# Turning the quantised silu product by DMA instead of on TensorE, with the down projection two tiles behind

## The chip, the cores and the metric

The kernel runs on one core of one Trainium2 chip. The metric is the device time of one execution in microseconds: a median of 1254.67 over three runs (1254.53 to 1255.34). Engines are named as in the profile: PE is TensorE, DVE is VectorE, ACT is ScalarE, POOL is GpSimd, SP is SyncE, which issues DMAs.

## The reference

Input is x (2 x 2048 x 512, fp32) and a context of 2 x 77 x 512. A causal cross-attention block of 16 heads comes first, `x = x + attention(layernorm(x), ctx)`, and then the feed-forward block, the one that is changed:

```
def fp4_quant_dequant(x):                      # blocks of 16 along the last dim
    xb = x.reshape(shape[:-1] + (shape[-1] // BLOCK, BLOCK))
    scale = jnp.maximum(jnp.max(jnp.abs(xb), axis=-1, keepdims=True) / 6.0, 1e-12)
    idx = jnp.searchsorted(_MID, jnp.abs(xb / scale))
    return (_GRID[idx] * jnp.sign(xb) * scale).reshape(shape)
def fp4_linear(x, w): return einsum('bsk,nk->bsn', fp4_quant_dequant(x), fp4_quant_dequant(w))
x = layernorm(x1)
h = silu(fp4_linear(x, w_gate)) * fp4_linear(x, w_up)    # 512 -> 1408
out = x1 + fp4_linear(h, w_down)                          # 1408 -> 512
```

The grid is 0, 0.5, 1, 1.5, 2, 3, 4, 6, with sign.

## The kernel before

All is done in 32 tiles of 128 rows (T = 32). The attention phase runs to about 461 us; it also quantises the weights, and leaves x1 and the turned down weights in DRAM. The feed-forward phase is `feed_forward`, a software pipeline written out by hand: each engine runs its own in-order list, `iteration(a)`, for a = 0 to T + 1, of which 4 to T - 2 are one hardware loop. Engines meet only through semaphores. There is no planner: the order of the lines is the order of the work.

Every matrix is carried as two fp32r parts, high and low, and each product is three matmuls (high x high, high x low, low x high). In iteration a TensorE computes gate and up of tile a in four chunks of 352 columns, each of 12 matmuls (`gate`, `up`), two PSUM banks for each. ScalarE takes silu of a gate chunk, VectorE multiplies it with the up chunk into `hid` (`gate_times_up`, L1188). Up of chunk c may start when the product of chunk c - 2 is made, gate of chunk c when silu of chunk c - 2 is done.

The product of tile a - 1 is quantised in iteration a on VectorE, with one step on ScalarE (class `Quant`): block maximum (L115), scale, its inverse and negated inverse, `divide` into z (L135), `shift` on ScalarE (L141), `make_magic`, `add_magic` (L150), `take_magic` (L155), which leaves grid values in fp32, and `rescale` (L161), which multiplies by the block scales into `hidq`. Between these steps stand the same steps for the input of tile a + 1 (`f.norm_stats` to `f.rescale`, 512 columns). TensorE then turns `hidq` in blocks of 128 x 128, in groups of 4, 4 and 3 (`transpose_hq`, L1096), into `hq_ps`; ScalarE copies each group to `hqh` (`hq_high`, L1155), and VectorE takes the rest to `hql` (`hq_low`, L1194). Both are single buffers of 128 x 11 x 128. `down(a - 1)` (L1099 to 1111) ends TensorE's iteration with 33 matmuls of 512 columns. The first copy of a tile has this wait ahead of it (L1148 to 1150), where t is a - 1:

```
                if g == 0:
                    if reached(t):
                        act.wait_ge(down_done, t)
```

VectorE adds the residual from `d_ps` (`add_residual`, L1201), SyncE stores the tile and loads the x1 rows of a later one (ring of 5). The next tile's input is turned by TensorE (`f.transpose`, L284), copied by ScalarE (`f.high`, L289) and VectorE (`f.low`, L293); gate of chunk 0 waits for both. Tiles 0 and T - 1 are quantised in two parts of 704 columns.

## Time and profile before

| what | value |
|---|---|
| median of three runs | 1254.67 us (1254.53 to 1255.34) |
| the profiled execution, span | 1252.7 us |
| instructions in it | 21798 |
| TensorE busy | 1224.3 us (98%) |
| VectorE busy | 1014.9 us (81%) |
| ScalarE busy | 466.5 us (37%) |
| GpSimd busy | 145.7 us (12%) |
| mean DMA rate | 47 GB/s |

The span runs from the first to the last recorded instruction of the profiled execution; the run's time is some 2 us longer than it. Busy matmul time overlaps: each matmul is listed at about 0.32 us (352 columns) or 0.39 us (512), while the next starts 0.16 or 0.23 us after it. So a cost on TensorE is read from one start to the next, and the other engines' from their durations.

### The profile page before, as it was taken

The numbers are of one execution on the slowest core, as the hardware profiler recorded it, in microseconds if no ns is written. First come the engines' busy times: TensorE is split into PE (matmuls) and PEld (weight loads), VectorE is DVE, ScalarE is ACT, GpSimd is POOL, SyncE is SP. The second block draws the span as 40 slices with busy tenths as digits, with TensorE's granted clock in tenths as the row PEclk, the third lists the DMA queues.
The fourth block names the chain that finished last, engine by engine and source line by source line (L and its number), as shares of the span: only waits on it lengthen the run. The fifth ranks groups of instructions, "written<-read, shape, count | busy, mean of one in ns | idle before, by whom it ended". The sixth has DMA issues, their size and how long they took to land.

```text
span 1252.7 us, 21798 instructions
## 1 busy us (share of the span) xinstructions
PE 1224.3 (98%) x7304; PEld 1119.5 (89%) x7304; DVE 1014.9 (81%) x1842; ACT 466.5 (37%) x1142; POOL 145.7 (12%) x239
## 2 busy tenths in 40 slices
PE   6899999999999989999999999999999999999998
PEld 4688888888888879999999999999999999999997
DVE  6899999989999948886887788688778877886875
ACT  3465656565656532222222232222222222322221
POOL 2011111111111100100100010011001000100100
PEclk9899999999999989999999999999999999999999
DMA  6112121211323242010000000000000100010000
GB/s 233 20 51 76 50 75 51 67 59 59 118 84 126 76 164 89 17 35 17 17 29 21 17 17 33 17 17 17 33 17 17 33 17 17 17 33 17 8 17 17
DMA packets 35666, 59.37 MB, mean 47 GB/s; under 512 B 5447, under 2 KB 11087, under 8 KB 35510
## 3 DMA queue, kind: packets, MB, share of 16 engines
q1 hardware_dynamic: 35638, 59.01, 13.9%
q8 instruction: 16, 0.26, 0.1%
q14 instruction: 12, 0.10, 0.0%
HBM read 36.13 MB, written 22.54 MB: 47 GB/s over the span
## 4 chain that ended last, share of the span: by engine, by line
PE 62%; DVE 1%; issue 0%; ACT 0%; DVEq 0%; ACTq 0%
PE g_ps L170 7%; PE g_ps L171 7%; PE g_ps L172 7%; PE u_ps L170 6%; PE u_ps L172 6%; PE u_ps L171 6%; PE d_ps L1108 6%; PE d_ps L1110 6%; PE d_ps L1109 6%; PE hq_ps L1096 3%; PE xn_ps L284 1%; DVE hql L1194 0%; DVE hquant_z L155 0%; DVE hquant_z L150 0%; DVE y L1201 0%
## 5 line engine op out<-in xcount | busy, mean ns | idle before, releaser
L1188 DVE TENSOR_TENSOR hid<-u_ps,silu 128x352 f32<-128x352 f32 x128 | 66.7, 521 | 142.4 <-PE u_ps L172 142.4
L170 PE MATMUL g_ps<-wguh,xnh 128*128 128x352 f32 x512 | 168.0, 328 | 3.7 <-PEq L299 2.2
L170 PE MATMUL u_ps<-wguh,xnh 128*128 128x352 f32 x512 | 167.3, 327 | 0.0
L171 PE MATMUL g_ps<-wgul,xnh 128*128 128x352 f32 x512 | 165.5, 323 | 0.0
L172 PE MATMUL g_ps<-wguh,xnl 128*128 128x352 f32 x512 | 165.3, 323 | 0.0
L172 PE MATMUL u_ps<-wguh,xnl 128*128 128x352 f32 x512 | 164.8, 322 | 0.0
L171 PE MATMUL u_ps<-wgul,xnh 128*128 128x352 f32 x512 | 164.7, 322 | 0.0
L754 ACT ACTIVATE probs<-s_ps,nsmax 128x77 f32<-128x77 f32 x512 | 114.1, 374 | 119.9 <-DVE nsmax L838 119.9
L1144 ACT ACTIVATE silu<-g_ps 128x352 f32<-128x352 f32 x128 | 58.9, 461 | 253.2 <-PE g_ps L172 253.2
L1108 PE MATMUL d_ps<-wd,hqh 128*128 128x512 f32 x352 | 140.3, 398 | 0.0
L1110 PE MATMUL d_ps<-wd,hql 128*128 128x512 f32 x352 | 137.3, 390 | 0.0
L1109 PE MATMUL d_ps<-wd,hqh 128*128 128x512 f32 x352 | 137.1, 389 | 0.0
L170 PEld LDWEIGHTS g_ps<-wguh,xnh 128*128 128x128 f32 x512 | 96.2, 188 | 5.7 <-issue 2.8
L171 PEld LDWEIGHTS g_ps<-wgul,xnh 128*128 128x128 f32 x512 | 96.3, 188 | 1.1
L171 PEld LDWEIGHTS u_ps<-wgul,xnh 128*128 128x128 f32 x512 | 96.3, 188 | 0.0
L170 PEld LDWEIGHTS u_ps<-wguh,xnh 128*128 128x128 f32 x512 | 96.2, 188 | 0.0
L172 PEld LDWEIGHTS g_ps<-wguh,xnl 128*128 128x128 f32 x512 | 96.2, 188 | 0.0
L172 PEld LDWEIGHTS u_ps<-wguh,xnl 128*128 128x128 f32 x512 | 96.1, 188 | 0.0
L243 POOL TENSOR_TENSOR nmean<-f_mv,minus_one 128x1 f32<-128x1 f32 x32 | 6.1, 190 | 687.1 <-DVE f_mv L238 687.1
L662 PEld LDWEIGHTS o_ps<-vbd,probsT 128*128 128x128 f32 (+1 forms) x640 | 76.5, 191 | 4.4
L1110 PEld LDWEIGHTS d_ps<-wd,hql 128*128 128x128 f32 x352 | 66.1, 188 | 14.4
L1155 ACT ACTIVATE hqh<-hq_ps 128x512 fp32r<-128x512 f32 (+1 forms) x96 | 53.9, 561 | 64.3 <-PE hq_ps L1096 64.3
(128 smaller groups left out, 2618.1 us busy)
## 6 DMA issues: line engine op xcount, KB each, us to landing
xin<-in_x_dram SPq DMA_DIRECT2D x32, 256.0 KB, 2.8
x_dram<-x SPq DMA_DIRECT2D x32, 256.0 KB, 2.0
xin<-x_dram SPq DMA_DIRECT2D x32, 256.0 KB, 2.8
out_dram<-y SPq DMA_DIRECT2D x32, 256.0 KB, 2.0
wd_dram<-wd_out SPq DMA_DIRECT2D x11, 512.0 KB, 3.6
wd<-wd_dram SPq DMA_DIRECT2D x1, 5632.0 KB, 17.1
w_in<-in_L_ffn_w_gate_dram SPq DMA_DIRECT2D x11, 256.0 KB, 2.9
w_in<-in_L_ffn_w_up_dram SPq DMA_DIRECT2D x11, 256.0 KB, 2.9
```

Of the source, the lines that this page charges most:

```text
L170: pe.matmul(out, lh, rh, start=(i == 0), stop=False)
L171: pe.matmul(out, lh, rl, start=False, stop=False)
L172: last = pe.matmul(out, ll, rh, start=False, stop=(i == n - 1))
L662: last = pe.matmul(o_ps[:, half, h0 * VW:(h1 + 1) * VW], probsT[0:rows, i, :], vbd[0:rows, b, half, c, 0:(h1 - h0 + 1) * VW], start=(c == ...
L754: last = act.activation(probs[:, h * CTX:(h + 1) * CTX], s_ps[:, bank, o:o + CTX], ACT.Exp, bias=nsmax[:, h:h + 1], scale=SCALE)
L1096: transposed = pe.transpose(hq_ps[:, g % 2, c - c0, :], hidq[:, c * P:(c + 1) * P], ident[:])
L1108: pe.matmul(d_ps[:], hqh[:, c, :], wd[:, 0, c, :], start=(c == 0), stop=False)
L1109: pe.matmul(d_ps[:], hqh[:, c, :], wd[:, 1, c, :], start=False, stop=False)
L1110: summed = pe.matmul(d_ps[:], hql[:, c, :], wd[:, 0, c, :], start=False, stop=(c == FC - 1))
L1144: act.activation(silu[:, c % 2, :], g_ps[:, c % 2, 0:GU_N], ACT.Silu).then_inc(silu_ready, 1)
L1155: act.activation(hqh[:, c0:c1, :], hq_ps[:, g % 2, 0:c1 - c0, :], ACT.Copy).then_inc(hqh_ready, 1)
L1188: dve.tensor_tensor(hid[:, c * GU_N:(c + 1) * GU_N], u_ps[:, c % 2, 0:GU_N], silu[:, c % 2, :], ALU.mult).then_inc(hid_ready, 1)
```

## The change

The product of tile t, for all tiles but the last, is no longer turned on TensorE. VectorE's last rounding step writes the grid values (exact in bf16) to `hg`; one transposing DMA from SyncE turns `hg` into `hgt`. The block scales (88 per row) are reordered by ScalarE, turned by TensorE in one instruction, copied from PSUM by ScalarE, stored to DRAM, and read back by eight broadcasting DMAs into `scale_wide`. VectorE multiplies `hgt` and `scale_wide` into `hqf`, ScalarE copies that to `hqh`, VectorE takes the difference to `hql`: each is now one instruction of 1408 columns. `down(a - 2)` takes the place of `down(a - 1)`, so the pipeline is one iteration longer. The turn of the next input moves ahead of up of chunk 3, `add_residual` of tile a - 3 moves ahead of the input's block maximum. Tile 0 is quantised whole. The last tile keeps the old way, in two parts, with its high and low parts in the space of the gate weights. GpSimd's own loop becomes the common one, with the same work for each tile. The core of the diff (declarations of semaphores, the signature, and longer runs of lines that only go left out; these stand in the listing above):

```diff
-        hidq = sb("hidq", [P, FF])
+        hqf = sb("hqf", [P, FC, P])
         hqh, hql = sb("hqh", [P, FC, P], F32R), sb("hql", [P, FC, P], F32R)
         y = sb("y", [P, 2, E])
         hquant = Quant(ctx, nc, "hquant", FF)
+        hg = sb("hg", [P, FF], BF16)
+        hgt = sb("hgt", [P, FC, P], BF16)
+        scale_cols = sb("scale_cols", [P, FB])
+        scale_rows = sb("scale_rows", [FB, P])
+        scale_wide = sb("scale_wide", [P, FC, P])
...
+        END = T - 1
+        lasth, lastl = (w[:, 0, 0:FF].rearrange("p (c k) -> p c k", k=P) for w in (k.wguh, k.wgul))
...
+        def looped(t):
+
+            return not isinstance(t, int) or 0 <= t < END
+
+        def is_end(t):
+            return isinstance(t, int) and t == END
+
+        LAST = T + 2
...
+            def scales_out(t):
+                sp.wait_ge(rows_ready, t + 1)
+                sp.dma_start(st_dram.rearrange("b (c k) -> (b c) k", k=P), scale_rows[:]).then_inc(rows_stored, 16)
+
+            def grid_transposed(t):
+                sp.wait_ge(hquant.grid_ready, t + 1)
+                if reached(t):
+                    sp.wait_ge(hqf_ready, t)
+                sp.dma_start_transpose(hgt[:], hg[:]).then_inc(hgt_loaded, 16)
+
+            def scales_in(t):
+                sp.wait_ge(rows_stored, 16 * (t + 1))
+                for b in range(P // BLK):
+                    sp.dma_start(scale_wide[b * BLK:(b + 1) * BLK, :, :].rearrange("p c k -> p (c k)"),
+                                 st_dram[b:b + 1, :].to_broadcast([BLK, FF])).then_inc(wide_loaded, 16)
+
...
...
+            for a in range(T + 3):
+                if looped(a - 1):
+                    scales_out(a - 1)
+                if valid(a - 3):
+                    store(a - 3)
+                    if a - 3 + RING < T:
+                        f.load(sp, a - 3 + RING, x1_t[a - 3 + RING])
+                if looped(a - 1):
+                    grid_transposed(a - 1)
+                    scales_in(a - 1)
...
...
+            def scales_transposed(t):
+                pe.wait_ge(cols_ready, t + 1)
+                if reached(t):
+                    pe.wait_ge(rows_ready, t)
+                pe.transpose(hq_ps[0:FB, 0, 0, :], scale_cols[:], ident[:]).then_inc(rows_done, 1)
+
+            def last_transposed(g):
+                pe.wait_ge(last_ready, 1 if g == 0 else 2)
+                if g < 2:
+                    pe.wait_ge(rows_ready, END)
+                else:
+                    pe.wait_ge(lastl_ready, g - 1)
                 c0, c1 = HQ_GROUPS[g]
                 for c in range(c0, c1):
-                    transposed = pe.transpose(hq_ps[:, g % 2, c - c0, :], hidq[:, c * P:(c + 1) * P], ident[:])
-                transposed.then_inc(hqT_done, 1)
+                    transposed = pe.transpose(hq_ps[:, g % 2, c - c0, :], hquant.z[:, c * P:(c + 1) * P], ident[:])
+                transposed.then_inc(lastT_done, 1)
 
...
+                high, low = (lasth, lastl) if is_end(t) else (hqh, hql)
                 for g, (c0, c1) in enumerate(HQ_GROUPS):
-                    pe.wait_ge(hqh_ready, NG * t + g + 1)
-                    pe.wait_ge(hql_ready, NG * t + g + 1)
+                    if is_end(t):
+                        pe.wait_ge(lasth_ready, g + 1)
+                        pe.wait_ge(lastl_ready, g + 1)
+                    elif g == 0:
+                        pe.wait_ge(hqh_ready, t + 1)
+                        pe.wait_ge(hql_ready, t + 1)
                     for c in range(c0, c1):
-                        pe.matmul(d_ps[:], hqh[:, c, :], wd[:, 0, c, :], start=(c == 0), stop=False)
-                        pe.matmul(d_ps[:], hqh[:, c, :], wd[:, 1, c, :], start=False, stop=False)
-                        summed = pe.matmul(d_ps[:], hql[:, c, :], wd[:, 0, c, :], start=False, stop=(c == FC - 1))
+                        pe.matmul(d_ps[:], high[:, c, :], wd[:, 0, c, :], start=(c == 0), stop=False)
+                        pe.matmul(d_ps[:], high[:, c, :], wd[:, 1, c, :], start=False, stop=False)
+                        summed = pe.matmul(d_ps[:], low[:, c, :], wd[:, 0, c, :], start=False, stop=(c == FC - 1))
...
             def iteration(a):
                 if valid(a):
                     gate(a, 0)
                     up(a, 0)
+                if looped(a - 1):
+                    scales_transposed(a - 1)
+                if valid(a):
                     gate(a, 1)
                     up(a, 1)
                     gate(a, 2)
-                if valid(a):
                     up(a, 2)
-                if valid(a - 1):
-                    transpose_hq(a - 1, 0)
-                if valid(a):
                     gate(a, 3)
...
                 if valid(a + 1):
                     f.transpose(pe, a + 1)
-                if valid(a - 1):
-                    transpose_hq(a - 1, 2)
-                    down(a - 1)
+                if valid(a):
+                    up(a, 3)
+                if is_end(a - 1):
+                    last_transposed(0)
+                    last_transposed(1)
+                if valid(a - 2):
+                    down(a - 2)
+                if is_end(a - 1):
+                    last_transposed(2)
 
...
...
+            def turn_scales(t):
+
+                act.wait_ge(hquant.scale_ready, t + 1)
+                if reached(t):
+                    act.wait_ge(rows_done, t)
+                act.activation(scale_cols[:].rearrange("p (b c) -> p b c", c=FC),
+                               hquant.scale[:].rearrange("p (c b) -> p b c", c=FC), ACT.Copy).then_inc(cols_ready, 1)
+
+            def scale_rows_out(t):
+                act.wait_ge(rows_done, t + 1)
+                if reached(t):
+                    act.wait_ge(rows_stored, 16 * t)
+                act.activation(scale_rows[:], hq_ps[0:FB, 0, 0, :], ACT.Copy).then_inc(rows_ready, 1)
+
+            def hq_high(t):
+                act.wait_ge(hqf_ready, t + 1)
+                if reached(t):
+                    act.wait_ge(down_done, t)
+                act.activation(hqh[:], hqf[:], ACT.Copy).then_inc(hqh_ready, 1)
+
+            def last_high(g):
+                act.wait_ge(lastT_done, g + 1)
                 c0, c1 = HQ_GROUPS[g]
-                act.activation(hqh[:, c0:c1, :], hq_ps[:, g % 2, 0:c1 - c0, :], ACT.Copy).then_inc(hqh_ready, 1)
+                act.activation(lasth[:, c0:c1, :], hq_ps[:, g % 2, 0:c1 - c0, :], ACT.Copy).then_inc(lasth_ready, 1)
 
             def iteration(a):
                 if valid(a + 1) and reached(a):
                     f.centre(act, a + 1)
-                if valid(a - 1):
-                    hquant.shift(act, quantised(a - 1), LAST_PART if split(a - 1) else ALL)
+                if looped(a - 1):
+                    turn_scales(a - 1)
+                    hquant.shift(act, a)
+                if is_end(a - 1):
+                    hquant.shift(act, T + 1, LAST_PART)
                 if valid(a + 1) and reached(a):
                     xquant.shift(act, PIECES + a + 2)
                 if valid(a):
...
+                    silu_of_gate(a, 0)
+                if looped(a - 1):
+                    scale_rows_out(a - 1)
+                if valid(a):
+                    silu_of_gate(a, 1)
+                    silu_of_gate(a, 2)
+                if looped(a - 1):
+                    hq_high(a - 1)
+                if is_end(a):
+                    hquant.shift(act, T, FIRST_PART)
                 if valid(a):
                     silu_of_gate(a, 3)
-                if valid(a - 1):
-                    hq_high(a - 1, 1)
                 if valid(a + 1):
                     act.wait_ge(up_done, GU * (a + 1))
                     f.high(act, a + 1)
-                if valid(a - 1):
-                    hq_high(a - 1, 2)
+                if is_end(a - 1):
+                    for g in range(NG):
+                        last_high(g)
 
...
-            def hq_low(t, g):
-                dve.wait_ge(hqh_ready, NG * t + g + 1)
+            def grid(t):
+
+                dve.wait_ge(hquant.sum_ready, t + 1)
+                if reached(t):
+                    dve.wait_ge(hgt_loaded, 16 * t)
+                dve.scalar_tensor_tensor(out=hg[:], in0=hquant.magic[:], scalar=ULP_FLOOR, in1=hquant.z[:],
+                                         op0=ALU.max, op1=ALU.subtract).then_inc(hquant.grid_ready, 1)
+
+            def hq_full(t):
+                dve.wait_ge(hgt_loaded, 16 * (t + 1))
+                dve.wait_ge(wide_loaded, 16 * (P // BLK) * (t + 1))
+                dve.tensor_tensor(hqf[:], hgt[:], scale_wide[:], ALU.mult).then_inc(hqf_ready, 1)
+
+            def hq_low(t):
+                dve.wait_ge(hqh_ready, t + 1)
+                dve.tensor_tensor(hql[:], hqf[:], hqh[:].bitcast(F32), ALU.subtract).then_inc(hql_ready, 1)
+
+            def last_low(g):
+                dve.wait_ge(lasth_ready, g + 1)
                 c0, c1 = HQ_GROUPS[g]
-                dve.tensor_tensor(hql[:, c0:c1, :], hq_ps[:, g % 2, 0:c1 - c0, :], hqh[:, c0:c1, :].bitcast(F32),
-                                  ALU.subtract).then_inc(hql_ready, 1)
+                dve.tensor_tensor(lastl[:, c0:c1, :], hq_ps[:, g % 2, 0:c1 - c0, :], lasth[:, c0:c1, :].bitcast(F32),
+                                  ALU.subtract).then_inc(lastl_ready, 1)
+
+            def quantise_last(part, done):
+                hquant.block_max(dve, hid[:], part)
+                hquant.block_scale(dve, done, part=part)
+                hquant.invert(dve, done, part=part)
+                hquant.negate(dve, done, part=part)
+                hquant.divide(dve, done, hid[:], part)
+
+            def round_last(part, done):
+                hquant.make_magic(dve, done, part)
+                hquant.add_magic(dve, done, part)
+                hquant.take_magic(dve, done, part)
+                hquant.rescale(dve, done, hquant.z[:], part).then_inc(last_ready, 1)
 
...
-                h, x = valid(a - 1), valid(a + 1) and reached(a)
-                part, done = LAST_PART if split(a - 1) else ALL, quantised(a - 1)
+                h, x = looped(a - 1), valid(a + 1) and reached(a)
+                done = a
                 if h:
-                    hquant.block_max(dve, hid[:], part)
+                    hquant.block_max(dve, hid[:])
                 if x:
                     f.norm_stats(dve, a + 1)
                 if h:
...
+                    if reached(a - 1):
+                        dve.wait_ge(cols_ready, a - 1)
+                    hquant.block_scale(dve, done)
+                    hquant.invert(dve, done)
+                    hquant.negate(dve, done)
+                    hquant.divide(dve, done, hid[:])
+                if is_end(a - 1):
+                    quantise_last(LAST_PART, T + 1)
+                if valid(a - 3):
+                    add_residual(a - 3)
                 if x:
                     f.block_max(dve, a + 1)
                     f.invert(dve, a + 1)
                     f.divide(dve, a + 1)
                 if h:
...
+                    hquant.make_magic(dve, done)
+                    hquant.add_magic(dve, done)
                 if x:
                     xquant.make_magic(dve, PIECES + a + 2)
                 if h:
-                    hquant.take_magic(dve, done, part=part)
+                    grid(a - 1)
                 if x:
                     xquant.add_magic(dve, PIECES + a + 2)
                 if valid(a):
                     gate_times_up(a, 0)
...
                 if x:
                     xquant.take_magic(dve, PIECES + a + 2)
                     f.rescale(dve, a + 1)
                 if valid(a):
                     gate_times_up(a, 1)
-                if split(a):
-                    first = quantised(a, FIRST_PART)
+                    gate_times_up(a, 2)
+                if h:
+                    hq_full(a - 1)
+                    hq_low(a - 1)
+                if is_end(a):
                     dve.wait_ge(hid_ready, GU * a + 2)
...
+                    dve.wait_ge(cols_ready, END)
+                    quantise_last(FIRST_PART, T)
+                    round_last(FIRST_PART, T)
+                if valid(a):
                     gate_times_up(a, 3)
...
                 if valid(a + 1):
                     f.low(dve, a + 1)
-                if valid(a - 1):
-                    hq_low(a - 1, 2)
+                if is_end(a - 1):
+                    round_last(LAST_PART, T + 1)
+                    for g in range(NG):
+                        last_low(g)
                 if valid(a):
                     dve.wait_ge(hid_ready, GU * (a + 1))
```

## Rows read from the trace of the kernel before

**Rows 1.** The page, part 1: busy time of each engine.
```profile
PE 1224.3 (98%) x7304; PEld 1119.5 (89%) x7304; DVE 1014.9 (81%) x1842; ACT 466.5 (37%) x1142; POOL 145.7 (12%) x239
```

**Rows 2.** TensorE's waits, 580 us to the end: us in total, times, longest.
```profile
PE hq_ps L1096 <- DVE hql L1194: 0.7, 1, 0.7
PE hq_ps L1096 <- DVE hidq L161: 0.2, 1, 0.2
```

**Rows 3.** Timeline of TensorE, start of tile 1: start us, us [idle before].
```profile
479.05 0.40 PE L170 MATMUL g_ps<-wguh,xnh 128*128 128x352 f32 x1 [1.52 <-ACT xnh L289]
```

**Rows 4.** Timeline of TensorE, start of tile 31.
```profile
1215.32 0.32 PE L170 MATMUL g_ps<-wguh,xnh 128*128 128x352 f32 x1
```

**Rows 5.** Timeline of VectorE over one tile, 618 to 634.2 us.
```profile
618.48 0.53 DVE L1188 TENSOR_TENSOR hid<-u_ps,silu 128x352 f32<-128x352 f32 x1 [3.21 <-PE u_ps L172]
618.92 0.68 DVE L1194 TENSOR_TENSOR hql<-hq_ps,hqh 128x512 fp32r<-128x512 f32 x1
619.52 0.68 DVE L293 TENSOR_TENSOR xnl<-xn_ps,xnh 128x512 fp32r<-128x512 f32 x1
620.12 0.55 DVE L1194 TENSOR_TENSOR hql<-hq_ps,hqh 128x384 fp32r<-128x384 f32 x1
620.58 1.61 DVE L115 TENSOR_REDUCE hquant_amax<-hid 128x88 f32<-128x1408 f32 x1
...
630.93 1.62 DVE L155 SCALAR_TENSOR_TENSOR hquant_z<-hquant_magic,hquant_z 128x1408 f32<-128x1408 bf16 x1
...
633.06 0.52 DVE L1188 TENSOR_TENSOR hid<-u_ps,silu 128x352 f32<-128x352 f32 x1
```

**Rows 6.** Timeline of TensorE, the down projection's first matmul and the next gate.
```profile
618.77 0.48 PE L1108 MATMUL d_ps<-wd,hqh 128*128 128x512 f32 x1
...
626.36 0.32 PE L170 MATMUL g_ps<-wguh,xnh 128*128 128x352 f32 x1
```

**Rows 7.** Timeline of TensorE around one group of turned blocks.
```profile
907.79 0.60 PE L1096 MATMUL hq_ps<-ident,hidq 128*128 128x128 f32 x4
908.15 0.41 PE L170 MATMUL g_ps<-wguh,xnh 128*128 128x352 f32 x1
908.39 0.33 PE L171 MATMUL g_ps<-wgul,xnh 128*128 128x352 f32 x1
```

**Rows 8.** Groups by line, 700 to 1180 us: busy us, mean ns, idle before.
```profile
L1096 PE MATMUL hq_ps<-ident,hidq 128*128 128x128 f32 x213 | 32.7, 272 | 0.0
L1155 ACT ACTIVATE hqh<-hq_ps 128x512 fp32r<-128x512 f32 (+1 forms) x58 | 32.6, 562 | 37.8 <-PE hq_ps L1096 37.8
...
L161 DVE TENSOR_TENSOR hidq<-hquant_z,hquant_scale 128x1408 f32<-128x1408 f32 x20 | 32.3, 1616 | 0.0
...
L141 ACT ACTIVATE hquant_magic<-hquant_z 128x1408 bf16<-128x1408 f32 x20 | 27.6, 1378 | 29.6 <-DVE hquant_z L135 29.6
```

**Rows 9.** Timeline of ScalarE, first silu of a tile.
```profile
628.69 0.45 ACT L1144 ACTIVATE silu<-g_ps 128x352 f32<-128x352 f32 x1
```

**Rows 10.** The page, part 6: DMA issues, KB each, us to landing.
```profile
xin<-x_dram SPq DMA_DIRECT2D x32, 256.0 KB, 2.8
out_dram<-y SPq DMA_DIRECT2D x32, 256.0 KB, 2.0
...
wd<-wd_dram SPq DMA_DIRECT2D x1, 5632.0 KB, 17.1
```

**Rows 11.** Timeline of VectorE, the last tile.
```profile
1233.36 0.88 DVE L115 TENSOR_REDUCE hquant_amax<-hid 128x44 f32<-128x704 f32 x1
...
1236.93 0.34 DVE L146 TENSOR_SCALAR hquant_magic<-hquant_magic 128x704 int16<-128x704 int16 x1 [0.86 <-ACT hquant_magic L141]
...
1239.23 0.89 DVE L161 TENSOR_TENSOR hidq<-hquant_z,hquant_scale 128x704 f32<-128x704 f32 x1
1240.04 0.68 DVE L1201 TENSOR_TENSOR y<-d_ps,xin 128x512 f32<-128x512 f32 x1
```

**Rows 12.** Busy time, granted clock (PEclk), DMA share, early stretches.
```profile
34.00:36.00 2.00, 1.85 (x8) 1.45 (x8) 1.39 (x3) 1.24 (x3) 0.00 (x0) 0.50 0.22 33
```

## Prediction of the time of the changed kernel

> **What bounds the kernel now.** Read the page's busy times first: TensorE is busy for 98% of the span [rows 1]. Then its waits from 580 us to the end: under 1 us in all, and both at the very end [rows 2]. In the feed-forward loop TensorE never waits, so a tile costs what its instructions cost. Tile 1 starts at 479.05 [rows 3] and tile 31 at 1215.32 [rows 4]: 736.27 / 30 = 24.54 us a tile. VectorE comes second, and what matters is where it starts in a tile. Its block maximum of the silu product starts at 620.58, while the down projection runs on TensorE from 618.77 to 626.36 [rows 5, 6]. VectorE has a head start of 5.8 us on the next gate matmul.
>
> **What leaves TensorE.** Four turns of the product begin at 907.79, a gate matmul follows at 908.15, but the next only at 908.39, where 0.16 is usual: 908.39 - 907.79 - 0.16 = 0.44 us for four, 0.11 each [rows 7]. (Their listed mean of 272 ns [rows 8] overlaps.) Eleven go, one comes, which alone costs about 0.17 with its change of operands: 1.21 - 0.17 = 1.04 us less per tile, 31 tiles, 32 us. That would be the whole effect if nothing else became late. The rest of the TensorE tile: a tile is 24.54 = 8 gate or up chunks + 15 turns x 0.11 + 7.59 of down projection (618.77 to 626.36), so a chunk is (24.54 - 1.65 - 7.59) / 8 = 1.91.
>
> **The wait that closes the loop.** ScalarE's copy hq_high(a-1) waits for down_done to reach a-1: the down projection of tile a-2 must be done, because hqh is one buffer. Before, that projection had been issued one iteration earlier, and the wait was met long ago. With the lag of two it is issued in the same iteration, as TensorE's last work. So hq_high starts only when TensorE has nothing left. Queued behind it on ScalarE: silu of chunk 3 and the copy of the next tile's input. Behind its result on VectorE, in this order: hq_low, the product of chunk 3, f.low. The next gate matmul waits for f.low. There is no deadlock (up of chunk 3 needs only the product of chunk 1), but the chain lies bare between two tiles:
> - drain of the last matmul, 0.16 (0.39 long, 0.23 apart), and 0.05 of signalling;
> - hq_high over 1408 columns. The nearest rows are 1.38 for 1408 columns to bf16, and 0.56 as the mean of 512 and 384 columns [rows 8]. I take 1.40;
> - hq_low, all from SBUF: 1.62 for 1408 columns of the same form [rows 8], 1.53 to the next start, with signal 1.55;
> - product of chunk 3, 0.45 to the next start, and f.low, 0.60 until VectorE goes on [rows 5].
>
> Together 0.21 + 1.40 + 1.55 + 0.45 + 0.60 = 4.2 us.
>
> **What is late next.** VectorE's head start is gone: its block maximum now starts with the gate matmuls, not 5.8 us ahead of them. From block maximum (620.58) to the end of the first product (633.06 + 0.52) is 13.0 us [rows 5], and the change keeps the operations in it: the residual moves earlier inside the same stretch, and the bf16 grid takes the place of take_magic at the same 1408 columns. Up of chunk 2 needs that product. TensorE gets there after 5 chunks and the turn of the scales: 9.55 + 0.17 = 9.7. It waits about 3.3 us. The 1.04 us saved lies partly ahead of this wait and is lost there.
>
> So the period of a tile: 13.05 (VectorE to the first product) + 3 x 1.91 + 0.44 (up 2, gate 3, turns of the input, up 3) + 7.59 (down) + 4.2 = 31.0; I take 31.1, so 6.56 more than 24.54. It holds for iterations 2 to 30, 29 of them: +190 us. ScalarE is no bound in it: it comes to silu of chunk 0 at 628.69, 8.1 after the block maximum [rows 9], and turning the scales (88 columns) fits ahead.
>
> **The DMA path.** After its grid VectorE has only the two quarters of the next input and three products to do before it multiplies. The grid ends at 630.93 + 1.62, 12.0 after block maximum. The transposed values need a latency D, then hq_full 1.62. As the copy to hqh waits anyway until 9.7 + 3.3 + 6.2 + 7.6 = 26.8, D costs nothing up to 13.2. Beyond, the loop is the DMA chain: 12.0 + D + 1.6 + 1.4 + 1.6 + 0.45 + 0.6, about 17.7 + D. No transposing DMA is in this trace. The nearest rows are 2.0 us for 256 KB and 17.1 for 5632 KB [rows 10]; the transfer is 352 KB. I take the row that is nearest by size, some 3 to 6 us with the queue: no cost. At the upper end, 17.1, the period is 34.8: 29 x 3.7 = 107 us more. Above 13.2 it pays, below zero it can't go, as nothing waits for it. The scales go beside it: rows out of PSUM at about 9, stored by 11, then eight broadcasts at some 0.4 of issue and 2.8 to landing [rows 10], there at about 18, well before 25.
>
> The page Advanced Engine Details and Errata of the Trainium skill, section X-Bar Transpose (TRN2), says that X-bar transposes are as fast as regular DMAs. Its sum would be the forecast. Against it speaks another page, DMA: Bandwidth & Descriptors, whose section Why a DMA increments its semaphore by 16 and not by 1 ends with a comparison that gives earlier generations 262,144 sequencer cycles for 8,192 tiles from SBUF to SBUF, 32 each. If a tile is a 256-byte piece, 1408 of them are 45,056 cycles, an estimate of 37 us at the 1.2 GHz that the Trainium skill's page Trainium Kernel Development and Optimization, section NeuronCore Architecture, gives SyncEngine: by the sum above about 2180 us. This trace shows neither.
>
> **First and last tiles.** Iteration 1 has no down projection, but VectorE's late product (13.0), 6.2 of TensorE, then hq_full, high and low wait for the scales at 18: about 23.8 against 24.5, -0.7. The end: iteration 31 has no next input, so its first product ends at 10.2; u2 to u3 and down(29) end at 23.6; copy and rest 3.2 to 26.8; then VectorE still has the first part of tile 31, 2.7 (1233.36 to about 1236.1) and, after ScalarE's shift, 3.2 (1236.93 to 1239.23 + 0.89) [rows 11]: 33.5. Product, last part 2.7, residual 0.7, 3.2: 40.8. Only then can the second group be turned, ahead of down(30). Two projections, turns, residual and store add 19.4: 60.2 after the start of tile 31, against 1252.7 - 1215.3 = 37.4. +22.8.
>
> **The clock.** Two idle stretches per tile, 4.2 and 3.3. In the trace of before the granted clock stands at 0.50 (1.2 GHz) from 34 to 36 us, in the setup, where TensorE had stood idle much of the time [rows 12]. [...] What falls after the gap between tiles lies ahead of the 3.3 us wait for VectorE and is paid by it. So 0 to 1.8 a tile; I take 0.3, 9 us in all, and 2.5 after the 17 us hole at the end.
>
> **Sum.** 1252.7 - 0.7 + 190 + 22.8 + 9 + 2.5 = 1476. The median of the runs, 1254.67, is 2 us above the profiled span: 1478 us.
>
> **Rivals.**
> 1. The transposing DMA takes more than 13 us and the loop is 17.7 + D: 1585 us at 17.1, more beyond. For it: an unseen kind of transfer, with 2-byte elements, on a queue where the eight broadcasts queue behind it. Against: the loop's own transfers land in 2.0 and 2.8 us [rows 10], and 13 us is much for 352 KB. 0.14.
> 2. The clock stays at 1.2 GHz for much of each tile: 1.8 x 29 = 52 more, 1530. For it: the two gaps. Against: TensorE is still busy for about 75% of a tile. 0.05.
> 3. Only one stall: the head start is kept in part, for instance because hq_low and the products overlap, and up 2 waits for nothing. Period 23.5 + 4.2 = 27.7: 29 x 3.2 + 25 = +118, 1373. Against: 13.0 on VectorE stands against 9.7 on TensorE [rows 5]. 0.04.
> 4. Faster: TensorE stays packed, because the copy's wait lets it run before the down projection of the same iteration. Price: -32 for the turns, +4 for the residual that now stands ahead of the last rounding: 1227. It decides where the idle time added to a tile is below 1.04 us. Against: the order of the lines, down(a-2) after up(a, 3) and one hqh. 0.04.
>
> **How the numbers follow.** The forecast has 0.72, rivals 0.27, and 0.01 is left for no change (within 0.2%, about 2.5 us, what can be told apart here). Its own range, ±0.6 a tile and D up to 14, is 1450 to 1530. I leave out rivals 3 and 4 below and the far part of rival 1 above: 1440 to 1600. Faster 0.04, same 0.01, slower 0.95.
>
> **What the changed profile would show.** TensorE's waits: g_ps at chunk 0 on VectorE's xnl, about 4.2 us, some 30 times; u_ps of chunk 2 on VectorE's product, about 3 us, 29 times. ScalarE: the copy to hqh released by the last down matmul. VectorE: hq_low right behind it. TensorE busy near 80%. One turn of 88 columns per tile. If the copy to hqh is released by VectorE's hqf, the DMA is the bound and rival 1 holds. If TensorE has no waits, the whole reading of down_done is wrong.

## The result, and the profile after

The changed kernel takes 1477.12 us (median of 4 runs, 1474.45 to 1479.21), against 1254.6: the ratio is 1.178, interval 1.176 to 1.181. Its profiled execution has a span of 1476.3 us. Forecast were 1478 us.

The page's busy times, which answer to [rows 1]:

```profile
PE 1269.5 (86%) x6994; PEld 1146.2 (78%) x6994; DVE 1012.0 (69%) x1771; ACT 462.8 (31%) x1141; POOL 104.0 (7%) x239
```

TensorE executes 310 matmuls fewer, and its busy share falls from 98% to 86% (near 80% was forecast). Its waits from 460 us on (us in total, times, longest) are these, where [rows 2] had under 1 us:

```profile
PE g_ps L171 <- DVE xnl L294: 118.8, 27, 4.4
PE u_ps L171 <- DVE hid L1252: 24.0, 26, 1.7
...
PE hq_ps L1134 <- DVE hquant_z L162: 15.8, 2, 9.8
```

They are the two forecast waits, between tiles and before up of chunk 2, and the hole at the end. The wait between tiles has a releaser in 27 tiles; in three more the trace names none. Timeline of VectorE over one tile (start us, us, idle before), which answers to [rows 5]:

```profile
908.58 1.63 DVE L1270 TENSOR_TENSOR hql<-hqf,hqh 128x1408 fp32r<-128x1408 f32 x1 [5.51 <-ACT hqh L1208]
910.12 0.52 DVE L1252 TENSOR_TENSOR hid<-u_ps,silu 128x352 f32<-128x352 f32 x1
910.56 0.68 DVE L294 TENSOR_TENSOR xnl<-xn_ps,xnh 128x512 fp32r<-128x512 f32 x1
911.16 1.61 DVE L116 TENSOR_REDUCE hquant_amax<-hid 128x88 f32<-128x1408 f32 x1
...
921.59 1.62 DVE L1260 SCALAR_TENSOR_TENSOR hg<-hquant_magic,hquant_z 128x1408 bf16<-128x1408 bf16 x1
...
923.74 0.52 DVE L1252 TENSOR_TENSOR hid<-u_ps,silu 128x352 f32<-128x352 f32 x1
...
932.77 1.62 DVE L1266 TENSOR_TENSOR hqf<-hgt,scale_wide 128x1408 f32<-128x1408 bf16 x1 [5.63 <-DMA scale_wide<-st_dram]
```

Timelines of ScalarE and of TensorE over the same tile; 906.69 is the last matmul of the down projection that ends the iteration before:

```profile
907.17 1.38 ACT L1208 ACTIVATE hqh<-hqf 128x1408 fp32r<-128x1408 f32 x1 [13.61 <-PE d_ps L1153]
...
938.37 1.38 ACT L1208 ACTIVATE hqh<-hqf 128x1408 fp32r<-128x1408 f32 x1 [13.52 <-PE d_ps L1153]
```

```profile
906.69 0.39 PE L1153 MATMUL d_ps<-wd,hql 128*128 128x512 f32 x1
911.48 0.65 PE L171 MATMUL g_ps<-wguh,xnh 128*128 128x352 f32 x1 [4.40 <-DVE xnl L294]
...
918.17 0.27 PE L1124 MATMUL hq_ps<-ident,scale_cols 128*88 128x128 f32 x1
...
924.31 0.43 PE L171 MATMUL u_ps<-wguh,xnh 128*128 128x352 f32 x1
...
930.60 0.40 PE L1151 MATMUL d_ps<-wd,hqh 128*128 128x512 f32 x1
...
937.89 0.39 PE L1153 MATMUL d_ps<-wd,hql 128*128 128x512 f32 x1
```

Read it as the chain it is. The last down matmul starts at 906.69; the copy to hqh at 907.17, after ScalarE has waited 13.61 us for it; hq_low at 908.58; the product of chunk 3 at 910.12; f.low at 910.56; the gate matmul at 911.48. VectorE's block maximum starts at 911.16, just before the gate and no longer 5.8 us ahead, so the first product ends at 924.26 (923.74 + 0.52), and up of chunk 2 starts at 924.31. SyncE's queue (start, us of issue):

```profile
920.57 0.29 SPq L1062 DMA_DIRECT2D st_dram<-scale_rows  x1
...
923.24 1.38 SPq L1068 DMA_TRANSPOSE hgt<-hg  x1
924.67 4.03 SPq L1073 DMA_DIRECT2D scale_wide<-st_dram  x8
```

From issue to landing the transposing DMA takes 3.9 us, and so does each broadcast. The list of DMAs, in the changed kernel and then in e1, where the same bytes go by a plain copy:

```profile
hgt<-hg SPq DMA_TRANSPOSE x31, 3.9
```

```profile
hgt<-hg SPq DMA_DIRECT2D x31, 352.0 KB, 2.7
```

VectorE has its data at 932.77, 5 us before the down projection ends at 938.

### The profile page after: what moved, and what is told of

The parts are those of the page before. It is cut to its first block, busy times and chain, and to the rows that moved or that the text cites. A ratio compares the mean times of both kernels' runs of the same rounds, so it can differ in the third digit from the quotient of the medians.

```text
span 1476.3 us, 21244 instructions
## 1 busy us (share of the span) xinstructions
PE 1269.5 (86%) x6994; PEld 1146.2 (78%) x6994; DVE 1012.0 (69%) x1771; ACT 462.8 (31%) x1141; POOL 104.0 (7%) x239
## 4 chain that ended last, share of the span: by engine, by line
PE 35%; DVE 19%; issue 9%; ACT 3%; DVEq 1%; SPq 0%; DMA 0%; ACTq 0%
PE d_ps L1151 5%; PE d_ps L1153 5%; PE d_ps L1152 5%; PE u_ps L171 4%; PE u_ps L172 3%; PE u_ps L173 3%; DVE hquant_z L151 3%; ACT hqh L1208 3%; DVE hquant_amax L116 3%; PE g_ps L171 2%; PE g_ps L173 2%; PE g_ps L172 2%; DVE hid L1252 2%; DVE hquant_inv L126 1%; DVE y L1295 1%
## 5 line engine op out<-in xcount | busy, mean ns | idle before, releaser
L171 PE MATMUL g_ps<-wguh,xnh 128*128 128x352 f32 x512 | 191.9, 375 | 139.4 <-DVE xnl L294 118.8
L171 PEld LDWEIGHTS g_ps<-wguh,xnh 128*128 128x128 f32 x512 | 111.1, 217 | 153.9 <-issue 150.2
L171 PE MATMUL u_ps<-wguh,xnh 128*128 128x352 f32 x512 | 179.4, 350 | 24.0 <-DVE hid L1252 24.0
L173 PE MATMUL g_ps<-wguh,xnl 128*128 128x352 f32 x512 | 185.1, 361 | 0.0
L172 PE MATMUL g_ps<-wgul,xnh 128*128 128x352 f32 x512 | 184.7, 361 | 0.0
L1208 ACT ACTIVATE hqh<-hqf 128x1408 fp32r<-128x1408 f32 x31 | 42.7, 1376 | 416.5 <-PE d_ps L1153 406.8
L1266 DVE TENSOR_TENSOR hqf<-hgt,scale_wide 128x1408 f32<-128x1408 bf16 x31 | 50.4, 1625 | 173.6 <-DMA scale_wide<-st_dram 173.6
L1270 DVE TENSOR_TENSOR hql<-hqf,hqh 128x1408 fp32r<-128x1408 f32 x31 | 50.4, 1625 | 164.7 <-ACT hqh L1208 164.7
L172 PEld LDWEIGHTS g_ps<-wgul,xnh 128*128 128x128 f32 x512 | 112.7, 220 | 0.0
L173 PEld LDWEIGHTS g_ps<-wguh,xnl 128*128 128x128 f32 x512 | 112.3, 219 | 0.0
```

The costliest lines, as they stand in the source:

```text
L171: pe.matmul(out, lh, rh, start=(i == 0), stop=False)
L172: pe.matmul(out, lh, rl, start=False, stop=False)
L173: last = pe.matmul(out, ll, rh, start=False, stop=(i == n - 1))
L1208: act.activation(hqh[:], hqf[:], ACT.Copy).then_inc(hqh_ready, 1)
L1266: dve.tensor_tensor(hqf[:], hgt[:], scale_wide[:], ALU.mult).then_inc(hqf_ready, 1)
```

## The experiments

Runs of the changed kernel are measured against 1477.1 us, those against the kernel before with their own runs of it beside them. A tile is the distance between two block maxima of the product, or its mean over many.

**Which wait bounds the loop: the down projection or the DMAs.** e1 takes the DMAs down:

```diff
-sp.dma_start_transpose(hgt[:], hg[:]).then_inc(hgt_loaded, 16)
+sp.dma_start(hgt[:].rearrange("p c k -> p (c k)"), hg[:]).then_inc(hgt_loaded, 16)
-for b in range(P // BLK): sp.dma_start(scale_wide[b * BLK:(b + 1) * BLK, ...], st_dram[b:b + 1, :]...)
+sp.dma_start(scale_wide[:].rearrange("p c k -> p (c k)"), st_dram[0:1, :].to_broadcast([P, FF]))
```

> The changed kernel with the transposing DMA replaced by a plain copy of the same bytes and the eight broadcasts by one of 128 rows (the values that reach the down projection are then not the reference's). Theory (the copy to hqh waits for the down projection of the same iteration, DMA hidden): VectorE's wait of 5.6 us per tile for scale_wide shrinks or goes and comes back as a longer wait for hqh; the tile stays at 31.2 us; only iteration 1, which has no down projection, gets some 3 to 5 us shorter: 1470 to 1477 us. Rival (the DMA path bounds the loop): VectorE's 5.6 us per tile come off, 1477 - 29 x 5.6 = 1315 us.

Measured: 1472.98 us. VectorE's waits, 480 to 1240 us:

```profile
DVE hql L1269 <- ACT hqh L1207: 234.7, 24, 10.5
...
DVE hqf L1265 <- DMA scale_wide<-st_dram: 23.3, 25, 1.1
```

The wait of 5.6 us for the data is down to 1, and the wait for the copy has grown from 5.5 to about 10. What one wait loses the next one gains, so the first was covered by the second, and the tile stays at 31.2. The 4 us are iteration 1, where nothing covers the DMAs: from gate to gate it takes 22.1 us (477.71 to 499.81) in place of 26.8.

e2 makes the path long: the transposing DMA is issued three times, each behind the one before. D is the time from the end of the grid operation to the data, as in the prediction.

> The changed kernel with the transposing DMA issued three times, each after the one before has landed, into the same tile: about 4 us more for each, so the data are there about 29.6 us after the block maximum, or D = 17.5 us behind the grid. Theory: up to D = 13.2 the DMA is free, beyond it the tile is 17.7 + D = 35.2 us, TensorE's copy then waits for hqf and not for the down projection: 1477 + 29 x 4.0 = 1593 us. Rival (DMA latency adds in full, as it would if it were in the chain already): 1477 + 29 x 8 = 1709 us.

Measured: 1573.06 us in a single run. Timeline of VectorE:

```profile
919.96 1.61 DVE L116 TENSOR_REDUCE hquant_amax<-hid 128x88 f32<-128x1408 f32 x1
...
930.41 1.63 DVE L1263 SCALAR_TENSOR_TENSOR hg<-hquant_magic,hquant_z 128x1408 bf16<-128x1408 bf16 x1
...
948.55 1.62 DVE L1269 TENSOR_TENSOR hqf<-hgt,scale_wide 128x1408 f32<-128x1408 bf16 x1 [12.59 <-DMA scale_wide<-st_dram]
...
954.19 1.61 DVE L116 TENSOR_REDUCE hquant_amax<-hid 128x88 f32<-128x1408 f32 x1
```

The tile is 954.19 - 919.96 = 34.23. The grid ends at 932.04, the data are there at 948.55: D = 16.5, and 17.7 + D = 34.2, as measured. The sum holds. The forecast of 1593 us had a tile of 35.2, as it took the two more DMAs for 8 us, and they cost 7. ScalarE's copy now waits for `hqf` in all 31 tiles, not for the down projection.

e8 tests the single buffer as the cause: two each of hqh and hql, the loop unrolled by two. The lines that matter:

```diff
-if reached(t): act.wait_ge(down_done, t)
+if reached(t - 1): act.wait_ge(down_done, t - 1)
-act.activation(hqh[:], hqf[:], ACT.Copy)
+act.activation(hqhs[hq_buf(t, 1)], hqf[:], ACT.Copy)      # hql and down() likewise
```

> The changed kernel with hqh and hql in two buffers each, used in turn, and nothing else moved: the copy of tile t waits for the down projection of tile t - 2. (To make room the low part of the down weights is left out and its matmuls read the high part, so that the work is the same and the values are not; the hardware loop takes two tiles a round.) Theory: the wait between tiles goes and the DMA chain is next, since hq_full, the copy, hq_low, product 3 and f.low still stand in a row behind it: scale_wide is there 21.6 us after the block maximum, plus 1.55 + 1.45 + 1.6 + 0.45 + 0.6 = 27.3 us a tile against 31.2: 1477 - 29 x 3.9 = 1364 us. Rival (the single buffer was the only fault): 23.5 us a tile, 1245 us.

Measured: 1360.05 us. Timeline of VectorE:

```profile
915.11 1.61 DVE L116 TENSOR_REDUCE hquant_amax<-hid 128x88 f32<-128x1408 f32 x1
...
936.72 1.63 DVE L1278 TENSOR_TENSOR hqf<-hgt,scale_wide 128x1408 f32<-128x1408 bf16 x1 [5.60 <-DMA scale_wide<-st_dram]
...
942.37 1.61 DVE L116 TENSOR_REDUCE hquant_amax<-hid 128x88 f32<-128x1408 f32 x1
```

A tile is 27.26, where 27.3 were expected. The data are there 21.6 us after the block maximum, as before, and nothing on ScalarE waits for a down projection any more: the DMAs are now the longer path. e9 then shortens the DMAs as e1 did, which alone had given 4 us:

> The kernel of e8 with the DMAs of e1 (a plain copy for the transposing DMA, one broadcast for eight; values not the reference's). In the changed kernel this is expected to give nothing. Theory (DMA chain is the bound once the buffer is doubled): the data are there some 16 to 17 us after the block maximum, the chain is 22 us, less than TensorE's 23.5: 1240 to 1260 us. Rival (the chain on VectorE is the bound whatever the DMAs do): as e8, within 10 us.

Measured: 1239.54 us, ratio 0.989 (0.986 to 0.991). Both edits together bring TensorE back to full. Either one alone leaves the kernel slower than before: 1473 us with the short DMAs, 1360 with the two buffers.

**VectorE's head start.** e3 moves the copy and the two operations around it behind the next tile's input:

```diff
 # ScalarE
-hq_high(a - 1)
 silu_of_gate(a, 3); f.high(act, a + 1)
+hq_high(a - 1)
 # VectorE
-hq_full(a - 1); hq_low(a - 1)
 gate_times_up(a, 3); f.low(dve, a + 1)
+hq_full(a - 1); hq_low(a - 1)
```

> The changed kernel with only the order moved: silu of chunk 3 and f.high ahead of the copy to hqh on ScalarE, product of chunk 3 and f.low ahead of hq_full and hq_low on VectorE. TensorE's wait of 4.4 us between tiles must go. Theory (VectorE's lost head start is the second bound): the block maximum now starts 3.2 us after the down projection ends, the first product is ready 16.2 us after the gate starts, where TensorE wants it at 9.7; one wait of 6.5 us takes the place of two. Tile 16.2 + 6.2 + 7.6 = 30.0 us: 1477 - 29 x 1.2 = 1442 us, and if the clock falls in that one long stretch and costs 1.7 us behind it, 1491 us; I take 1465. Rival (the wait between tiles is all): 4.4 us a tile come off, 1350 us.

Measured: 1438.42 us. TensorE's waits, 440 us to the end:

```profile
PE hq_ps L1124 <- ACT scale_cols L1195: 101.5, 30, 4.7
PE u_ps L171 <- DVE hid L1252: 37.9, 30, 1.8
```

The wait between tiles is gone, all of it, and 3.4 + 1.3 us a tile stand elsewhere: at the turn of the scales, which I had not seen (ScalarE's `turn_scales` and the step ahead of it wait for VectorE, whose block maximum now starts 3.2 us behind the gate; ScalarE is idle for 4.7 us after the copy), and before up of chunk 2, on the first product. Up of chunk 2 starts 16.4 us after the gate, 16.2 forecast; the first of the two waits is covered by the second. The tile is 30.2, forecast 30.0, and the time lies near the 1442 us of that sum; the 1465 that I took, with a part for a slow clock, missed. A wait of 4.4 us taken away gave 1.0.

**The clock.** e6 puts 18 unused matmuls behind each down projection:

```diff
+for _ in range(18):
+    pe.matmul(hq_ps[:, 1, :, :]..., k.wguh[:, 0, 0:P], wd[:, 0, 0, :], start=True, stop=True)
```

> The changed kernel with 18 unused matmuls of 512 columns behind each down projection but the last ones (4.1 us at full clock, into an unused PSUM bank), so that TensorE is not idle between tiles. The granted clock should stay at 1.00. Theory (what the clock costs lies ahead of the wait for the first product and is paid by it): the wait at u_ps grows from about 1 us to 3.3 us, the tile becomes at most 0.3 us shorter: 1468 to 1477 us. Rival (the fallen clock is a real part of the loss): at 0.933 mean clock over 1476 us, some 100 us of half speed, 1425 us.

Measured: 1475.72 us, clock 0.991 on average in the profiled run in place of 0.933. So 0.058 of clock are worth 1.4 us here, no more than the runs differ among themselves. What pays for it is seen in the changed kernel's busy times by stretch (length, PE, PEld, DVE, ACT, POOL, PEclk, DMA, GB/s):

```profile
907.00:911.00 4.00, 0.08 (x1) 0.00 (x0) 2.42 (x3) 2.21 (x3) 0.00 (x0) 0.96 0.00 0
911.00:913.00 2.00, 1.52 (x5) 1.53 (x6) 2.00 (x3) 0.00 (x0) 0.00 (x0) 0.50 0.00 0
...
915.00:917.00 2.00, 2.00 (x9) 2.00 (x8) 2.00 (x2) 0.69 (x2) 0.03 (x1) 0.50 0.00 0
...
919.00:921.00 2.00, 2.00 (x14) 2.00 (x13) 1.97 (x3) 1.52 (x4) 0.00 (x0) 1.00 0.00 0
```

TensorE was idle from 907.1 to 911.5, and most of the first two chunks then runs at 1.2 GHz: the scales are turned at 918.17, 6.7 us after the gate starts, where 24 matmuls at 0.16 are 3.85. That is 2.8 us lost, and TensorE comes to up of chunk 2 almost as the product is ready. In other tiles the slow stretch is shorter and the wait longer: in tiles 4 to 30 the scales are turned 5.3 to 6.8 us after the gate, and up of chunk 2 starts 12.8 us after it each time. Another tile of the changed kernel, its scales turned at 604.71, and one of e6:

```profile
599.22 0.42 PE L171 MATMUL g_ps<-wguh,xnh 128*128 128x352 f32 x1 [4.40 <-DVE xnl L294]
...
612.05 0.43 PE L171 MATMUL u_ps<-wguh,xnh 128*128 128x352 f32 x1 [1.34 <-DVE hid L1252]
```

```profile
907.17 0.42 PE L171 MATMUL g_ps<-wguh,xnh 128*128 128x352 f32 x1 [0.21 <-DVE xnl L294]
...
920.00 0.43 PE L171 MATMUL u_ps<-wguh,xnh 128*128 128x352 f32 x1 [1.69 <-DVE hid L1255]
```

All three have 12.8 us between the two rows: VectorE sets the time, whatever the clock. 0.9 us of listed wait are left in the changed kernel (24.0 us in 26 tiles). In e6 the waits are back, 50.3 us for the product in 31 tiles, and 24.5 for silu ahead of it. In tile 31, where no input is quantised and the product is ready early, the slow clock stands bare (see **The end** in the next section).

**A schedule that has neither wait.** e4 uses the lag of two for what it allows: `hq_full`, the copy and `hq_low` of tile a - 2 stand in the middle of iteration a. The copy's wait is then met by the down projection of the iteration before.

```diff
 # VectorE, ahead of the next input's block maximum
+hq_full(a - 2)
 # ScalarE and VectorE, between chunks 1 and 2
+hq_high(a - 2)          # ScalarE
+hq_low(a - 2)           # VectorE
 # SyncE, ahead of the store of the scales
+sp.wait_ge(wide_loaded, 16 * (P // BLK) * t)
-hq_high(a - 1) / hq_full(a - 1); hq_low(a - 1)
```

> The changed kernel with hq_full, the copy to hqh and hq_low of tile a - 2 (not a - 1) in the middle of iteration a, all buffers single as they are. The copy then waits for the down projection of the iteration before, which is done, and VectorE does not wait for the DMAs. Theory: both waits go and TensorE is packed again; the tile is 24.54 - 1.04 = 23.5 us: 1254.6 - 31 x 1.04 + about 4 at the end (residual ahead of the last rounding) = 1227 us, clock 1.00. Rival (DMA traffic or the one turn costs TensorE more than the row of before says, or VectorE is too late for the first product with 1.6 us more ahead of it): 1245 to 1270 us.

Measured: 1252.19 us, ratio 0.998 (0.997 to 0.999). The forecast of 1227 missed; the time lies in the rival's range. TensorE's waits and VectorE's residual:

```profile
PE hq_ps L1136 <- DVE hquant_z L162: 8.0, 1, 8.0
PE u_ps L171 <- DVE hid L1255: 5.0, 12, 1.7
```

```profile
880.90 1.61 DVE L116 TENSOR_REDUCE hquant_amax<-hid 128x88 f32<-128x1408 f32 x1
...
887.61 0.69 DVE L1298 TENSOR_TENSOR y<-d_ps,xin 128x512 f32 x1 [1.35 <-PE d_ps L1155]
...
904.74 1.61 DVE L116 TENSOR_REDUCE hquant_amax<-hid 128x88 f32<-128x1408 f32 x1
```

A tile is 23.84, 23.9 in most. The residual, which the change had moved ahead, waits 1.35 us for the down projection that is still running, and TensorE comes to up of chunk 2 some 0.4 us before its product (0.54 from one matmul's start to the next where 0.16 is usual; the trace lists a wait for it in 12 tiles only). At the end the last tile's groups hold up a down projection that is ready. e5 mends both by order alone; its lines for ScalarE and VectorE in the last iterations are left out here.

```diff
+elif looped(a - 2): hq_full(a - 2)
 hquant.add_magic(dve, done)
+if valid(a - 3) and not is_end(a - 1): add_residual(a - 3)
 # TensorE, iteration T
 last_transposed(0)
-last_transposed(1)
 down(a - 2)
+last_transposed(1)
 last_transposed(2)
```

> The kernel of e4 with two more moves of order: the residual of tile a - 3 goes back behind add_magic, where it stood before, and at the end hq_full, the copy to hqh and hq_low of tile 30 and its down projection come ahead of the last tile's second and third group. In e4 VectorE waited 1.35 us a tile for the down projection at the residual, TensorE then 0.3 us for the first product, and TensorE stood 8.0 us idle ahead of the last groups. Theory: both go, the tile is 23.5 us: 1252 - 29 x 0.33 - 8 = 1234 us. Rival (the time of e4 is DMA traffic or the longer pipeline as such): 1245 to 1252 us.

Measured: 1235.64 us, ratio 0.986 (0.984 to 0.987): faster than both kernels. Of the 20.2 us between the profiled runs of e4 and e5, 13.4 lie between the first block maximum of a whole product and the last, 5.7 behind the last and 1.1 ahead of the first. Neither move was run alone.

The block maxima of two tiles, 18 apart:

```profile
707.37 1.61 DVE L116 TENSOR_REDUCE hquant_amax<-hid 128x88 f32<-128x1408 f32 x1
```

```profile
1129.85 1.61 DVE L116 TENSOR_REDUCE hquant_amax<-hid 128x88 f32<-128x1408 f32 x1
```

(1129.85 - 707.37) / 18 = 23.47 against 24.54. Single tiles run from 23.34 to 23.65, and the 23.63 named in a later expectation was one of them.

**What the turns cost.** e7 puts ten turns back into e5:

```diff
+for g in range(10):
+    pe.transpose(hq_ps[:, 1, g % 4, :], ident[:], ident[:])
```

> The kernel of e5 with ten more turns of 128 x 128 behind the one turn of the scales, of the identity into an unused PSUM bank: what the change took from TensorE comes back, with nothing else. Theory (a turn costs TensorE 0.11 us, nothing hides it): 31 x 10 x 0.11 = 34 us: 1270 us. Rival (a turn hides in the pipeline or costs its listed 0.27 us): 1236 or 1320 us.

Measured: 1265.84 us (1260.53 to 1270.03), 30.2 us more: 0.10 a turn. The runs spread over 10 us, so the tile is the better measure:

```profile
715.85 1.61 DVE L116 TENSOR_REDUCE hquant_amax<-hid 128x88 f32<-128x1408 f32 x1
```

```profile
1107.31 1.61 DVE L116 TENSOR_REDUCE hquant_amax<-hid 128x88 f32<-128x1408 f32 x1
```

16 tiles of 24.47, 1.00 more than e5: again 0.10 a turn, in a run of ten; in the groups of four of [rows 7], 0.11.

e10 gives e5 the DMAs of e1.

> The kernel of e5 with the DMAs of e1 (a plain copy for the transposing DMA, one broadcast for eight; values not the reference's). In e5 a tile takes 23.63 us with TensorE never waiting, in e9 23.34. Theory (the small packets of the transposing DMA or of the broadcasts slow the matmuls a little): 0.3 us a tile come off, 1227 us. Rival (the 0.3 us have another source, such as which rows the down projection reads in e9): 1236 us.

Measured: 1233.66 us, interval of the ratio 0.983 to 0.986 beside e5's 0.984 to 0.987. Its tiles are 23.47 (706.53 to 1129.01), those of e9 23.48: the difference of 0.3 us that the expectation set out from was one between single tiles, and the rival of 1236 us fits. The small packets of these DMAs cost TensorE nothing in the loop; a loop without any DMA was not run.

## Why the prediction was right, step by step

- **The wait that closes the loop** was right as a mechanism, and nearly so in its price. Counted as the prediction counts, from 0.23 us after the last down matmul's start to the gate, it is 4.6 us where 4.2 were forecast (911.48 - 906.69 - 0.23; the trace lists 4.4 of it as idle). The terms fit: copy 1.38 (1.40), hq_low 1.54 to the next start (1.55), product 0.44 (0.45), f.low 0.60. What the sum left out is the last step, from where VectorE goes on (911.16) to the gate (911.48), 0.3. A second buffer (e8) and the copy moved to where the projection is done (e4) show the wait as the cause.
- **VectorE's head start** was right: 13.1 us from block maximum to first product (13.0), up of chunk 2 12.8 us after the gate. The form of the wait was off: 3.3 us were forecast, 0.9 stand there, and the rest is slow clock ahead of it. The prediction had said that the clock would be paid from this wait, and then added 0.3 us a tile, 9 us in all. No row and no run shows that term, nor the 0 to 1.8 that it was picked from: in the loop the slow clock costs 1.4 to 2.9 us a tile ahead of the wait, and nothing of the tile (e6).
- **The tile**: 31.1 + 0.3 forecast; from the gate of tile 2 to that of tile 31, (1410.94 - 505.63) / 29 = 31.22 measured, 5.3 us less over the loop. In parts it is 12.8 to up of chunk 2, 6.3 to the down projection (924.31 to 930.60; 6.2 forecast), 7.5 of that (7.6) and 4.6:

```profile
478.84 0.40 PE L171 MATMUL g_ps<-wguh,xnh 128*128 128x352 f32 x1 [1.46 <-ACT xnh L290]
...
505.63 0.63 PE L171 MATMUL g_ps<-wguh,xnh 128*128 128x352 f32 x1 [7.99 <-issue]
```

```profile
1410.94 0.63 PE L171 MATMUL g_ps<-wguh,xnh 128*128 128x352 f32 x1 [4.26 <-issue]
```

- **The DMA path**: no cost in the loop, as forecast, but for the wrong reason in part. The transposing DMA lands after 3.9 us. The data are late all the same, 9.6 us behind the grid and not 3 to 6: the scales were taken to be there at 18, and are there at 21.6, because their eight broadcasts (4.0 us of issue) stand in SyncE's queue behind the transposing DMA (1.4), which waits for the grid. The loop has room for it: `hqf` is complete 23.2 us after the block maximum (932.77 + 1.62 - 911.16), and the copy may start only at 27.2 (938.37). Iteration 1 has none: 505.63 - 478.84 = 26.8 us in place of 23.8. The Trainium skill's page Advanced Engine Details and Errata, section X-Bar Transpose (TRN2), says that X-bar transposes are as fast as regular DMAs. The runs agree only roughly: the same 352 KB land after 2.7 us as a plain copy in e1, and after 3.9 by the transposing DMA. Both are far from the 37 us that the prediction had set against it.
- **The end** was mis-sized by 2.7: 65.4 us from the gate of tile 31 (1410.94 to 1476.3) where 60.2 + 2.5 were forecast.

```profile
1446.14 1.12 PE L1134 MATMUL hq_ps<-ident,hquant_z 128*128 128x128 f32 x4 [9.79 <-DVE hquant_z L162]
1453.30 1.12 PE L1134 MATMUL hq_ps<-ident,hquant_z 128*128 128x128 f32 x4 [6.04 <-DVE hquant_z L162]
...
1465.20 0.50 PE L1151 MATMUL d_ps<-wd,wguh 128*128 128x512 f32 x1 [1.77 <-DVE y L1295]
```

```profile
1452.00:1456.00 4.00, 2.70 (x9) 2.31 (x10) 2.50 (x4) 0.60 (x1) 0.00 (x0) 0.50 0.00 0
```

The second group is turned 42.4 us after that gate, not 40.8. That is the slow clock, and not VectorE: tile 31 has no next input ahead of its product, so up of chunk 2 waits for nothing and starts 12.0 us after the gate, with the scales turned at 6.2. In e6 the clock is full there, up of chunk 2 starts after 10.2 us and the group is turned after 40.6 (1406.52 to 1447.13), which is the forecast. Then the last down projection waits 1.8 us for the residual of the one before, as both use `d_ps`: a wait that the prediction had left out. The clock is at 0.50 behind the hole, as forecast, but costs less: from the second group to the third 9.65 us pass (1453.30 to 1462.95) where 0.44 + 7.5 is full speed, an estimate of 1.7 for the 2.5 of the sum, which no row had shown. Together 1.6 + 1.8 - 0.8 = 2.6 of the 2.7.
- **The turns**: 1.04 us a tile forecast, 24.54 - 23.47 = 1.07 measured where TensorE does not wait (e5), and 1.00 for ten of them in e7. The prediction's remark that part of the saving lies ahead of the wait for VectorE and is lost there is a misreading: `transpose_hq` stood behind up of chunk 2 each of the three times, and only the one turn that is added stands ahead. Its sum had the order right. That one turn was put at 0.17 and costs 0.11 (918.44 - 918.17 - 0.16, with 918.44 the second gate matmul behind it). In the changed kernel the two waits cost several times what the turns give.

Together: -0.2 (up to tile 1), +3.0 (iteration 1), -5.3 (loop), +2.7 (end): the span was forecast as 1476 and is 1476.3, because the errors cancel. That both come to the same microsecond is luck; that they lie within some 10 us is not, as the loop's period was right to 0.2 us.

**The rivals.** The long DMA is excluded by e1 for this kernel, and e2 shows that the loop would follow it if it were long. The clock rival is excluded by e6. Only one stall: excluded by the 12.8 us from gate to up of chunk 2 in the changed kernel's trace, and by e3, where taking the first stall away gives 1.0 us and not 4.4. A packed TensorE: it takes e5, not this order.

## What to carry to other kernels

When work is put off by one more iteration, list for each single buffer who frees it and when in the new order; a wait that had long been met can become the last event of the iteration, and all that stands behind it on two in-order engines becomes bare. Price a new gap by the loop it closes, not by its length: 4.4 us taken away gave 1.0 (e3), and 4.6 us of DMA wait taken away gave nothing in the loop (e1) until the buffer was doubled (e9). Here the lag bought time only when the late operations were moved into it (e5), and then the change's own idea, ten turns fewer, was worth its 1.07 us a tile.

## What was not expected of the hardware

A mean granted clock of 0.933 in place of 0.991 cost 1.4 us of 1477, which is within the spread of the runs (e6): the slow stretches followed TensorE's own idle time and fell where it would have waited again. Where no such wait stood it cost 1.8 us in tile 31, and by estimate 1.7 behind the hole at the end. A turn of 128 x 128 fp32 costs 0.10 to 0.11 us of TensorE's time though it is listed with 0.27. Eight broadcasts of 88 KB take 4.0 us of issue on SyncE's queue, the transposing DMA of 352 KB 1.4, a plain copy of the same bytes 0.47 (e1).
